# A two-layer graph network: engines wait for the stores between the layers themselves, read the count of long tiles before they wait, and six feature loads move ahead of the last store

## The reference

```python
h = relu(layernorm(x))
q, k, v = h @ Wq + bq, h @ Wk + bk, h @ Wv + bv
alpha = segment_softmax(einsum(q[dst], k[src]) / sqrt(C), dst)
x = x + segment_sum(v[src] * alpha, dst) + (h @ Wskip + bskip)      # this is x1
h = relu(layernorm(x))
h_self, hh = split(h @ W_kernel + W_bias)
send = (hh[src] + edge_attr @ We_kernel + We_bias) * in_degree[dst]
x = x + h_self + segment_sum(send, dst)
```

## Time and profile before

| | us |
|---|---|
| median of 3 runs | 1664.47 |
| lowest and highest run | 1663.79, 1665.09 |
| span of the profiled execution, first to last instruction | 1662.8 |
| first gather of layer 2, end of its last | 1010.0, 1636.0 |
| last output store issued, all output in | 1652.5, 1654.1 |

### The profile page before, as it was taken

One profiled execution on the slowest core, in us unless ns is written; L12 is line 12 of the kernel. 1 busy time (PEld: TensorE's weight loads), 2 busy tenths in 40 slices (PEclk: granted clock), 3 DMA queues, 4 the chain that ended last, 5 costly groups with the idle time before them and its releaser, 6 DMA issues. The chain is left out here.

```text
span 1662.8 us, 34477 instructions
## 1 busy us (share of the span) xinstructions
PE 1470.4 (88%) x10545; PEld 1263.5 (76%) x10546; DVE 1347.6 (81%) x3688; ACT 1016.5 (61%) x2501; POOL 1083.1 (65%) x1202
## 2 busy tenths in 40 slices
PE   5888898699999999999999974899998999998996
PEld 4666777688888888888888863777776777777775
DVE  8879665299999999999999994677776777777675
ACT  5777888556555565656665513566665666665663
POOL 2554442577777777777777605777777777777772
PEclk9999999899999999999999996999999999999999
DMA  8899887556666666666666516677666767667672
GB/s 219 274 274 313 284 300 262 157 160 180 189 174 192 175 188 183 178 182 182 182 174 185 156 45 148 148 160 174 162 163 150 171 160 172 161 158 170 149 164 68
DMA packets 162552, 302.85 MB, mean 182 GB/s; under 512 B 104113, under 2 KB 107703, under 8 KB 157524
## 3 DMA queue, kind: packets, MB, share of 16 engines
q1 hardware_dynamic: 121503, 201.19, 41.9%
q0 software_dynamic: 40896, 99.90, 24.9%
HBM read 196.84 MB, written 104.12 MB: 181 GB/s over the span
## 5 line engine op out<-in xcount | busy, mean ns | idle before, releaser
L803 POOL DMA_INDIRECT sb_kv<-kv_rows,sb_src_all x500 | 492.9, 986 | 187.1 <-issue 131.3
L831 POOL DMA_INDIRECT sb_kv<-x_rows,sb_src_all x500 | 473.8, 948 | 209.3 <-issue 109.1
L1710 ACT ACTIVATE sb_hn<-sb_xn 100x128 f32<-100x128 f32 x500 | 240.5, 481 | 265.9 <-DMA sb_kv<-x_rows,sb_src_all 225.1
L1713 ACT ACTIVATE sb_vw<-sb_kv 128x128 f32<-128x128 f32 x500 | 239.6, 479 | 0.0
L1638 ACT ACTIVATE sb_hn<-sb_xn,sb_nstat 100x128 f32<-100x128 f32 x500 | 231.5, 495 | 0.0
L1400 DVE COPY sb_hT<-ps_b 128x400 f32<-128x400 f32 x250 | 142.2, 569 | 96.1 <-PE ps_b L2005 95.3
L1797 PE MATMUL ps_b<-sb_w,sb_memberT 128*125 128x256 f32 x800 | 201.6, 391 | 18.3 <-DVE sb_xn L921 9.2
L1660 ACT COPY sb_memberT<-ps_b 100x512 f32<-100x512 f32 x150 | 75.8, 506 | 205.7 <-PE ps_b L1885 205.7
L1797 PEld LDWEIGHTS ps_b<-sb_w,sb_memberT 128*125 128x125 f32 x800 | 146.2, 193 | 41.7 <-issue 14.7
L2005 PE MATMUL ps_b<-sb_member,sb_vw 128*128 128x100 f32 x1000 | 173.8, 278 | 0.0
L2005 PEld LDWEIGHTS ps_b<-sb_member,sb_vw 128*128 128x128 f32 x1000 | 157.4, 198 | 9.8 <-issue 9.8
(11 more groups left out here) (184 smaller groups left out, 3103.0 us busy)
## 6 DMA issues: line engine op xcount, KB each, us to landing
kv_rows<-sb_kv SPq DMA_DIRECT2D x26, 1120.0 KB
sb_xn<-x_rows SPq DMA_DIRECT2D x50, 507.8 KB
sb_xn<-in_x SPq DMA_DIRECT2D x50, 500.0 KB
out_rows<-sb_xo SPq DMA_DIRECT2D x49, 500.0 KB
x_rows<-sb_xo SPq DMA_DIRECT2D x24, 1015.6 KB
sb_kv<-in_edge_attr SPq DMA_DIRECT2D x500, 32.0 KB
sb_kv<-in_x SPq DMA_DIRECT2D x28, 560.0 KB
kv_rows<-sb_xn SPq DMA_DIRECT2D x13, 1120.0 KB
```

What stands on the lines that cost most here:

```text
L803: pool.indirect_dma_start(out=kvs[:, k % 4, t, :], out_offset=None, in_=kv_rows, in_offset=bass.IndirectOffsetOnAxis(ap=src_all[:, n:n + 1 ...
L831: pool.indirect_dma_start(out=xs1[:, k % 4, t, :], out_offset=None, in_=x1, in_offset=bass.IndirectOffsetOnAxis(ap=src_all[:, n:n + 1], ax ...
L1710: nc.scalar.activation(hn1[:, t, :], xn1[:, k % 4, t, 0:D], ACT.Relu, scale=xn1[:, k % 4, t, D:D + 1], bias=xn1[:, k % 4, t, D + 1:XW]).th ...
L1713: nc.scalar.activation(hs1[:, t, :], xs1[:, k % 4, t, 0:D], ACT.Relu, scale=xs1[:, k % 4, t, D:D + 1], bias=xs1[:, k % 4, t, D + 1:XW]).th ...
```

## The change

Four things change. In `long_tiles` the wait for the stores and the raising of the loop's semaphores move into the branch that is taken only where there are long tiles; the count is read and the branch decided before any of it. At the end of that branch, in layer 1, SP raises `long_done[0]` and the engines wait for it. Behind `long_tiles` of layer 1, each engine waits for the x1 stores itself (`stored_all(..., 0)`) in place of `long_done[0]`. Behind `long_tiles` of layer 2, SP alone waits for the output stores; the other four engines leave the block without that wait. And `features` takes a range of tiles: its first six loads for batch 0 stand ahead of the last x1 store, with the window registers loaded one step earlier, and the other four where all ten stood.

```diff
@@ def long_tiles
-            eng.reg_mov(cursor, 0)
-            eng.reg_mov(chunks, 1)
-            stored_all(eng, S.n)
-            for primed, by in S.first[eng.engine.name]:
-                eng.sem_inc(primed, by)
             with eng.If(count > 0):
+                eng.reg_mov(cursor, 0)
+                eng.reg_mov(chunks, 1)
+                stored_all(eng, S.n)
+                for primed, by in S.first[eng.engine.name]:
+                    eng.sem_inc(primed, by)
                 with eng.Fori(1, count + 1) as i:
...
+                if S.n == 0 and eng.engine.name == "SP":
+                    eng.sem_inc(long_done[0], 1)
+                if S.n == 0:
+                    eng.wait_ge(long_done[0], 1)
@@ SP
+            def features(k, found, first=0, last=B):
+                if k == 0 and first == 0:
+                    sp.wait_ge(A.vw, BATCHES)
+                wait(sp, R.ae, 2 * (k - 3))
+                for t in range(first, last):
+                    sp.dma_start(eaw[:, k % 4, t, 0:DE], ea[bass.ds(found[t], WIN), :]).then_inc(R.ea[k % 4], 16)
...
-                if k == BATCHES:
+                if k == BATCHES - 1:
                     first_windows = window_registers(0)
                 if k >= 1 and real(k + 1):
                     segments(k + 1)
+                if k == BATCHES + 1:
+                    features(0, first_windows, 0, 6)
                 if k >= 3 and k % 2 == 1:
                     store((k - 3) // 2)
...
-            features(0, first_windows)
+            features(0, first_windows, 6, B)
             long_tiles(sp, S0, long_rows(S0, x, D), long_edges(S0), long_store(S0, x1, XW))
-            sp.sem_inc(long_done[0], 1)
-            sp.wait_ge(long_done[0], 1)
+            stored_all(sp, 0)
...
             long_tiles(sp, S1, long_rows(S1, x1, XW), long_edges(S1), long_store(S1, out, D))
+            stored_all(sp, 1)
@@ POOL (and DVE, ACT, PE alike)
             long_tiles(pool, S0, None, long_gather(S0, x, D), None)
-            pool.wait_ge(long_done[0], 1)
+            stored_all(pool, 0)
```

More of the change, by code:

```diff
@@ L683, in long_store @@
                 return after
[L685 to L690, removed]
             def nodes1(k):
@@ L1581, in _ @@
             long_tiles(dve, S0, long_node_stats(S0), long_chunk0, long_finish0)
-            dve.wait_ge(long_done[0], 1)
+            stored_all(dve, 0)
             dve.wait_ge(ones_set, 2)
@@ L1758, in _ @@
             long_tiles(act, S0, long_turned_rows(S0), long_chunk0, None)
-            act.wait_ge(long_done[0], 1)
+            stored_all(act, 0)
             for k in range(BATCHES):
@@ L2103, in _ @@
             long_tiles(pe, S0, long_rows_projected(S0), long_chunk0, None)
-            pe.wait_ge(long_done[0], 1)
+            stored_all(pe, 0)
             pe.wait_ge(ones_set, 2)
```

## The result

| | before | after |
|---|---|---|
| median of 6 runs each, us | 1664.82 | 1655.41 |
| lowest and highest, us | 1663.79, 1665.89 | 1652.86, 1659.76 |
| ratio, with its 95% interval | | 0.9935 (0.9917 to 0.9952) |
| span of the profiled execution, us | 1662.8 | 1652.2 |

The kernel became faster by 9.4 us in the median, and by 10.8 us by the ratio (8.0 to 13.8). The runs of after spread over 7 us, which the forecast had not allowed for.

The account below looks back on a forecast made before the run. POOL's gathers were taken to bound layer 2: first gather's start plus 626.0 us plus a fixed tail. Gains of 3.6 us (seam) and 8.2 us (end) sum to 11.8, from 1664.47 to 1652.7 us; range 1650.8 to 1657.6.

Parts of the forecast that it names:

- The seam: Between the layers: own waits on the x1 stores start layer 2's first gather 3.6 us sooner, between 2.7 and 3.9.
- The six loads: Ahead of the last x1 store: SP issues them in 5.3 us, over by about 998.5, with 1.5 us of cover.
- The traffic: Packets of the six loads ahead of the last x1 store: cost taken as 0, 0.9 us as the bad end.
- The gathers: Layer 2: POOL's 500 gathers at 1.25 us each take 626.0 us and never wait for a buffer.
- The drain: POOL after its last gather: 8.24 us, over near 1642.3, hidden with over 8 us of cover before the last output store.
- The end: After the last output store: the span ends 0.5 us behind it instead of 8.7; gain 8.2 us, between 7.2 and 8.4.
- The lower end of the range, 7.2: Kernel's end: smallest gain expected there, allowing 1 us for SP leaving its block by an unconditional branch after its wait.
- The fixed tail: After layer 2's last gather: a constant stretch, added to the first gather's start plus 626.0 us to give layer 2's end.
- The drain did leave the path: Rival at the kernel's end: POOL's drain stays on the path, only the seam gains, 1660.9 us; chance 0.09.
- the seam's gain was not given back: Rival in layer 2: SP's feeding holds it, the seam's gain is lost, only the tail's 8.2 us remain, 1656.3 us; chance 0.07.
- PE's clock was back at its higher level: Rival in layer 2: PE's clock stays at its lower level after the seam, 1668 us or more; chance 0.03.

Follow-up runs that it names:

- e3: The kernel before with only the six feature loads moved ahead of the last x1 store, flag and end kept; 1662.71 us against 1667.06, ratio 0.9967.
- e4: The changed kernel with all ten feature loads back behind the last x1 store; 1654.45 us against 1667.06 before, ratio 0.9918.
- e11: The changed kernel with a POOL drain added behind layer 2's last gather, then a POOL wait for the output stores; one run, 1655.96 us.
- e6: The changed kernel with two POOL drains in a row added after layer 1's last gather; one run, 1656.82 us against 1668.73 before.
- e12: The changed kernel with three of ten feature matmuls done twice in batches 0 to 45 of layer 2; 1653.45 us against 1667.29 before, ratio 0.9915.

## Why the prediction was right, and where it was off

The forecast was 1652.7 us, 11.8 below before. The median of after is 1655.41, within the range; the places that were edited gave 10.8 us in the profile.

- **The seam: right, 3.57 us for 3.6.** POOL is released by the stores, 6.6 us after DVE's last step. By e3 and e4, the forecast was right to give the whole gain to the own waits and nothing more to the loads.
- **The six loads: mis-sized.** They took 6.67 us where 5.3 was reckoned, from the rates of ten loads behind the last store. The first four took 5.4 us and not 4.29, the other two 1.3 and not 1.0. They ended at 1000.75, 0.7 us before the last store, not 1.5. The cover held, but closely; had it not, SP would have been late for the store that all wait for. The traffic, taken as 0 with 0.9 us as the bad end, cost nothing: 6.62 us from the statistics to the gather with the moved loads, 6.55 without. The Trainium skill (DMA: Bandwidth & Descriptors, section on queues, rings and completion order) says that an engine consumes a queue's descriptors in ring order; these two traces show no loss by it.
- **The gathers: right.** 625.3 us from the first start to the last end, for 626.0.
- **The drain: right, and off the path.** It ended 8.3 us behind the last gather. The forecast took it for fixed work behind gathers; e11 shows this for layer 2, and e6 that a second drain is free. The Trainium skill (VectorE: DVE Perf Modes, section "The DRAIN you can't avoid") gives about 12 ns, constant on all five engines, for the runtime's drains at a kernel's start and end. Of the drains of L143, with which the kernel's own block ends, SP's 7 ns before agree; POOL's take 47 ns once it has drained and 8242 ns behind gathers.
- **The end: mis-sized, 7.2 us for 8.2.** The way from the last store's issue to SP's branch was taken as 1.6 us, unchanged; it is 2.3 (1649.14 to 1651.48). From there to SP's drain it is 0.5 us, not 0.2. The lower end of the range, 7.2, had been set by the second of these alone.
- **The fixed tail: wrong as a rule.** The sum rested on layer 2's end being the start of the first gather plus 626 us plus a fixed tail. The tail is PE's lag, and goes from 15 to 21 us with where PE's clock last fell. In the two profiles that was at 1539 and 1538 and the tails were alike (17.5 and 16.9 us); by this luck the sum did not suffer. The three runs of before, 1.3 us apart, gave a far too narrow idea of the spread: in the next block the same kernel covered 14 us.
- **The rest of the difference.** The profile of after is 1.4 us late at layer 1's first gather, and the median of its runs lies 1.3 us above its profiled execution. That execution lies 1.9 us above its span, not 1.7. With the 1.0 us at the end, these are more than the 2.7 us by which the forecast was low; the 0.6 us of gathers and the 0.6 us of lag go the other way.
- **The rivals.** The drain did leave the path, the seam's gain was not given back, and PE's clock was back at its higher level by 1040 in every trace. But it falls again later, in the trace of before too (at 1051, 1266 and 1539); the mean of 0.99 from 1100 to 1600, on which the forecast leaned, hides such falls.

## What to carry to other kernels

An engine that issues gathers should be sent to its drain as soon as its last gather is issued; a wait put ahead of that drain puts all of its price behind the wait. Where many engines wait for a flag that only passes on a semaphore, let each wait for the semaphore itself, before moving work out of the way of the engine that raises the flag: the first made the second needless here. Where one engine sets the pace and PE is busy for 92% of it (11.5 of 12.5 us here), PE's clock can fall when PE catches up and has to wait, and the end then depends on how much of the lag is left; a distance in one profile is then one draw, and the spread wants more than three runs.

## What the runs showed of the hardware that was not expected

- POOL's drain takes 8.24 us behind layer 2's last gather, whether it is asked for at once or 18 us later, 4.6 us behind layer 1's, where it was asked for at once, and 47 ns when nothing was gathered since the last drain.
- Three extra matmuls a batch, 0.52 us in 12.5, kept PE's waits for ACT at 0.8 us or less and its clock at the higher level for 600 us of e12's trace, and cost nothing that could be measured.
- Six feature loads behind a 1 MB store took SP 6.67 us, 5.4 of it for the first four; of the ten that stood behind such a store before, the first four took 4.3 us and the last six 0.5 each.
